# A fused two-stage window attention and long-convolution kernel: entry and stage ends reordered, fewer fillers, the first attention block in four groups of whole rows

## The chip, the cores and the metric

The kernel runs on one core of a Trainium2 chip. The metric is device time in microseconds (us) of one execution; 220.42 us is the median of three runs of the kernel before (219.79 to 220.80). The engines are TensorE (PE in the profile; PEld is its weight load), VectorE (DVE), ScalarE (ACT), GpSimd (POOL) and SyncE (SP), which here only issues DMAs. Each engine works through its own program in order, and the programs meet at semaphores.

## The reference

The input x has 32 channels and 56 x 56 pixels. Two residual steps follow one another:

```python
def _gn(v, G=32, eps=1e-05):      # norm of each channel over its image
...
x = x + _L0_conv_ref(_gn(x), ...)  # two attention blocks
x = x + _L1_conv_ref(_gn(x), ...)  # long convolution, GLU, layer norm, decoder
```

The first step is a window attention (block stage, "b": 8 x 8 windows of 7 x 7 neighbouring pixels), then a grid attention (stage "g": 7 x 7 windows of 8 x 8 pixels). Each has 4 heads of 8 channels, a bias table by relative position, a softmax, a projection with residual, a layer norm over the 32 channels and a feed-forward of 128 with the norm's output as its shortcut. The second step encodes 32 channels to 256, convolves each with 16 taps that come from a small state-space model, applies GELU, a gated linear unit, a residual, a layer norm over 256, and decodes to 32 channels.

## The kernel before

**Stages.** The whole image lies in SBUF. The kernel goes through: entry (loads, first group norm, first q/k), block stage (to about 71 us), grid stage (to about 130 us), second group norm and the start of the convolution (to 136), convolution with GELU (to 165), GLU with norm and decoder in seven chunks of 448 pixels (to the end). To keep precision at half-precision matmul speed, many operands are split in a half-precision part ("hi") and a half-precision remainder ("lo").

**Entry.** The group norm takes its sums from `xq`, four quarters of x_win side by side (loads L416 on SP, L801 on ACT). DVE forms the statistics (L1082 to L1088), after it made the key tables, with two copies into `ones` (L1192). The selection table `sel` (L418, third in SP's queue) gives `repeat32` (L1199), with which PE sums the quarters (L1796). ACT turns the result into scale and offset `gr` (L824 to L829). Then `x1`, which comes in three pieces (PIECES, L40; loads L425 on SP for rows 0 to 63 and L808 on ACT for rows 64 to 95), is normed in four window pieces of 784 columns: ACT writes the hi copy (`window_hi`, L841), someone writes the full copy into `u32` (`window_f32`: DVE for piece 0, L1313, ACT for pieces 1 to 3, L847), and the lo part is their difference (`window_lo`: DVE for piece 0, POOL for pieces 1 to 3, L678). The q/k matmul of window row r (L1593) needs the lo part. POOL also makes the bias halves (`split_bias`, L542), which the scores need, and issues the loads of p1, par_g and w_glu.

**Attention in groups.** `strips` (L315) lists the groups: two strips of windows are worked on at once in the two halves of the partitions. In the block stage groups 0 to 2 hold two whole window rows (8 windows wide), groups 3 and 4 one window row each, cut in two halves of 4 windows. `groups`, `rows_of`, `halves_of` and the use of the PSUM banks (`ring_uses`, L354) follow from the list. For each group g PE's loop (L1822 to L1861) runs the second orientation of the scores of two heads (`turned_scores`, L1648), values, the projection of the group before, the scores of the next group, the other two heads, the variance of the group before, then the attention sums in one or two halves (`attend`, L1688), the q/k of later rows and the feed-forward of the group before. ACT's loop (L978 to L1009) runs exp (L885), the log and exp that invert the row sums (L898, L900), and the norm's square, log and exp (L913, L921, L928). DVE's loop (L1384 to L1427) takes the row maxima (L1225), the q/k splits (L1178), the outputs (L1255), the norm's output (L1266) and puts finished rows back in image order (L1285).

**Feed-forward.** `feed_forward` (L1742) uses two half-precision matmuls on the parts that POOL makes (`norm_halves`, L696) for all groups but the last, and one full-precision matmul for the last (L1762), so that no wait for POOL stands there.

**Fillers.** `keep_running(n)` (L1766) issues n matmuls of 512 columns on a zero tile, whose result is not used. They stand in places where PE would be idle.

**After the grid stage.** DVE's second group norm gives `gr`. The first chunk's shifted copies in `u4hi` are written by ACT (rows 0 to 63, L1022) and DVE (L1439), and the lo parts in `u4lo` by DVE (s = 0, 1, L1448) and POOL (s = 2, 3, L753). All later chunks are shifted by DMAs from `ust_s` (L449, L457, L760), in the segments of L39. At the end, for the last chunk, the order on PE is L2011 to L2018, with the sums of squares in `mean_square` (L1928) inside `decode(last)`, and DVE's is L1541 to L1546.

## Time and profile before

| | us |
|---|---|
| median of three runs | 220.42 |
| profiled execution, its own time | 220.49 |
| its span, first to last instruction | 218.7 |
| PE busy | 197.0 (90%) |
| DVE busy | 151.2 (69%) |
| ACT busy | 128.7 (59%) |
| POOL busy | 102.5 (47%) |
| all fillers on PE (114) | 34.8 |
| mean granted TensorE clock | 0.966 |

The profile comes from one execution; its time lies within the three runs. Busy shares are over the whole span. A wait is named after the instruction whose semaphore came last. In timeline rows the first two numbers are the start and the length of a merged run of instructions, the brackets hold the idle time before it and who ended it.

### The profile page before, as it was taken

To read this page: it belongs to the slowest core of one execution; us is meant where nothing else is said; L and a number is where in the kernel's file an instruction comes from. 1 tells how busy PE (TensorE), PEld (TensorE's weight loads), DVE (VectorE), ACT (ScalarE), POOL (GpSimd) and SP (SyncE) were. 2 spreads that over 40 slices of the span, in tenths; PEclk is the share of its full clock that TensorE was granted. 3 is DMA by queue.
4 is the path that set the end of the run, shared out by engine and by line. 5 is a ranking of instruction groups with operands and counts; after the bars stand their busy time and mean duration, and the time that the engine had idled before them with its cause. 6 is when DMAs were issued, how large, how long until landed. Compare 5 with 4: busy or idle time off the path is not lost.

```text
span 218.7 us, 6364 instructions
## 1 busy us (share of the span) xinstructions
PE 197.0 (90%) x2563; PEld 102.9 (47%) x2563; DVE 151.2 (69%) x300; ACT 128.7 (59%) x248; POOL 102.5 (47%) x221
## 2 busy tenths in 40 slices
PE   7698789989898799898989796999999999999995
PEld 2254334435553244344344343445555556666582
DVE  8777486947664676739878789963323768898873
ACT  2373986775574737765636619755448665656650
POOL 7258562737860313767895504410000466577540
PEclk9889999999999799999999999999999999999975
DMA  6765500000000000020000000460000000000000
GB/s 181 168 155 121 113 4 4 4 3 3 3 3 0 0 3 3 17 86 1 3 4 0 3 0 12 95 146 2 0 0 0 3 0 3 13 11 13 11 11 21
DMA packets 3841, 6.70 MB, mean 31 GB/s; under 512 B 1605, under 2 KB 2773, under 8 KB 3717
## 3 DMA queue, kind: packets, MB, share of 16 engines
q1 hardware_dynamic: 2581, 3.91, 7.8%
q0 software_dynamic: 560, 1.48, 2.7%
q10 hardware_dynamic: 672, 0.92, 1.7%
q8 instruction: 20, 0.33, 0.7%
q14 instruction: 8, 0.07, 0.1%
HBM read 4.53 MB, written 0.40 MB: 23 GB/s over the span
## 4 chain that ended last, share of the span: by engine, by line
PE 65%; DVE 13%; ACT 11%; issue 4%; POOL 3%; DMA 2%; SPq 0%; DVEq 0%; ACTq 0%; POOLq 0%
PE ps L1923 15%; PE ps L1888 13%; PE ps L1769 5%; PE ps L1683 3%; DVE x L1285 3%; PE ps L1727 3%; PE ps L1739 2%; DMA sel<-pick 2%; PE ps L1704 2%; PE ps L1661 2%; PE ps L1673 2%; PE ps L1629 2%; PE ps L1709 2%; PE ps L1974 2%; PE ps L1593 2%
## 5 line engine op out<-in xcount | busy, mean ns | idle before, releaser
L1769 PE MATMUL ps<-fill 128*128 128x512 f16 x114 | 34.8, 429 | 1.8 <-DVE fill L1355 1.2
L1225 DVE TENSOR_REDUCE mx<-ps 128x16 f32<-128x784 f32 (+3 forms) x18 | 15.8, 888 | 15.2 <-PE ps L1643 15.2
L885 ACT ACTIVATE pr<-ps 128x784 f32<-128x784 f32 (+3 forms) x18 | 13.7, 761 | 12.0 <-PE ps L1683 11.9
L858 ACT CAST q_hi<-ps 128x392 f16<-128x392 f32 (+1 forms) x30 | 13.8, 512 | 11.3 <-PE ps L1593 10.9
L768 POOL TENSOR_TENSOR pr<-pr 128x448 f16<-128x448 f32 x7 | 7.4, 1063 | 27.0 <-ACT pr L1064 27.0
L1769 PEld LDWEIGHTS ps<-fill 128*128 128x128 f16 x114 | 10.8, 107 | 14.7 <-issue 4.9
L1040 ACT ACTIVATE pt<-ps,ybias 128x448 f32<-128x448 f32 x14 | 8.9, 637 | 12.9 <-PE ps L1888 12.0
L1285 DVE STREAM_TRANSPOSE x<-u 96x448 f32<-96x448 f32 (+4 forms) x12 | 13.9, 1154 | 2.0 <-ACT u L938 1.7
L1923 PE MATMUL ps<-vm_buf,wglu_hi 128*128 128x448 f16 x56 | 15.1, 352 | 0.0
L1888 PE MATMUL ps<-u4hi,gw_hi 128*128 128x448 f16 x56 | 12.9, 353 | 1.5 <-ACT u4hi L1022 1.5
L1064 ACT CAST pr<-pr 128x448 f16<-128x448 f32 x14 | 7.9, 566 | 10.0 <-DVE pr L1519 10.0
L1467 DVE TENSOR_TENSOR vm_buf<-pt,qs 128x448 f16<-128x448 f32 x7 | 4.4, 624 | 13.3 <-ACT qs L1042 13.3
L692 POOL TENSOR_TENSOR ust_g<-x,ust_g 32x448 f16<-32x448 f32 x5 | 5.1, 1026 | 17.1 <-ACT ust_g L947 17.0
L1704 PE MATMUL ps<-pr,ones 128*32 128x196 f32 (+2 forms) x120 | 8.5, 354 | 5.1 <-DVE on L1255 3.8
L1888 PE MATMUL ps<-u4hi,gw_lo 128*128 128x448 f16 x56 | 12.9, 352 | 0.0
L1178 DVE SCALAR_TENSOR_TENSOR qs<-q_hi,cst,ps 128x392 f16<-128x392 f16 (+1 forms) x15 | 9.7, 646 | 4.4 <-ACT q_hi L858 4.1
L1888 PE MATMUL ps<-u4lo,gw_hi 128*128 128x448 f16 x56 | 11.7, 352 | 0.5 <-POOL u4lo L753 0.5
L1512 DVE SCALAR_TENSOR_TENSOR pt<-ps,p,pt 128x448 f32<-128x448 f32 x14 | 9.6, 683 | 3.4 <-ACT pt L1056 1.8
L773 POOL TENSOR_TENSOR pr<-pr 128x448 f32<-128x448 f32 x6 | 6.8, 1134 | 9.4 <-ACT pr L1065 9.4
L1255 DVE TENSOR_TENSOR on<-ps,rec 128x196 f32<-128x196 f32 (+2 forms) x15 | 5.6, 375 | 7.1 <-ACT rec L900 7.1
L898 ACT ACTIVATE den<-ps 128x196 f32<-128x196 f32 (+2 forms) x15 | 5.2, 349 | 8.9 <-PE ps L1709 8.7
L1519 DVE SCALAR_TENSOR_TENSOR pr<-ps,p,pt 128x448 f32<-128x448 f32 x14 | 9.6, 683 | 0.5
(275 smaller groups left out, 531.9 us busy)
## 6 DMA issues: line engine op xcount, KB each, us to landing
xr<-x SPq DMA_DIRECT2D x3, 392.0 KB, 5.5
wglu<-w_glu POOLq DMA_DIRECT2D x1, 512.0 KB, 4.4
x<-x_win SPq DMA_DIRECT2D x4, 112.0 KB, 3.9
out<-u SPq DMA_DIRECT2D x7, 56.0 KB, 1.6
x<-x_win SPq DMA_DIRECT2D x2, 168.0 KB, 5.2
u4hi<-ust_s SPq DMA_DIRECT2D x4, 84.0 KB, 2.6
par_g<-stage_g POOLq DMA_DIRECT2D x1, 274.5 KB, 3.1
x<-x_win ACTq DMA_DIRECT2D x2, 112.0 KB, 6.1
```

The costliest lines, as they stand in the source:

```text
L858: nc.scalar.copy(q_hi[:, i % 4, 0:cw], qk_bank(k, i)[:, 0:cw]).then_inc(s_qkhi[k], 1)
L885: nc.scalar.activation(dst[:, :, 0:cw], ps[:, 2:4, 0:cw], ACT.Exp).then_inc(s_exp[k], 1)
L1040: nc.scalar.activation(gy[n % 2][a], ps[:, i % 4, 0:CW], ACT.Gelu_apprx_tanh, bias=ybias[:, a:a + 1])
L1178: nc.vector.scalar_tensor_tensor(out=dst[:, r * cw:(r + 1) * cw], in0=q_hi[:, i % 4, 0:cw], scalar=const(low), in1=qk_bank(k, i)[:, 0:cw], ...
L1225: nc.vector.tensor_reduce(m[:, :, 0:n], ps[:, bank:bank + 2, 0:n * T].rearrange("p h (j m) -> p h j m", m=T), AX.X, ALU.max).then_inc(s_mx ...
L1285: nc.vector.transpose(x1[:, :].rearrange("p (c k) -> p k c", c=C)[:, first:last, :], u32[:, first * C:last * C].rearrange("p (k c) -> p k ...
L1512: nc.vector.scalar_tensor_tensor(out=ag[a], in0=ps[:, VALUE[a], 0:CW], scalar=s4("bglu")[:, a:a + 1], in1=sg[a], op0=ALU.add, op1=ALU.mult ...
L1519: nc.vector.scalar_tensor_tensor(out=rr[n % 2][a], in0=ps[:, ENC[a], 0:CW], scalar=s4("benc")[:, a:a + 1], in1=ag[a], op0=ALU.add, op1=ALU ...
L1704: nc.tensor.matmul(ps[32 * h:32 * h + 32, 6, 256:256 + w], weights, p[:, h, first * T:last * T], start=True, stop=True)
L1769: nc.tensor.matmul(ps[:, bank, :], fill[:, 0:128], fill[:, :], start=True, stop=True)
L1888: ins = nc.tensor.matmul(ps[:, i % 4, 0:CW], wt[:, j, a * 128:(a + 1) * 128], ut[:, at:at + CW], start=(first and j == 0), stop=(last and ...
L1923: ins = nc.tensor.matmul(ps[:, bank, 0:CW], wt[:, b, o:o + 128], yt[b][:, c], start=(m == 0), stop=(m == 5))
```

## The change

It touches ten places.

1. SP issues the load of `sel` before its two quarters, and no longer loads rows 0 to 63 of piece 1; POOL does, behind its memsets and ahead of its wait for piece 0, on a semaphore of its own.
2. The window pieces: piece 0's hi copy is made in two halves on ACT, and its lo part in two halves on DVE; the full copy of piece 1 is made on POOL, in front of `split_bias("b")`; ACT makes hi copy 2 and full copy 2 ahead of the group loop, and hi copy 3 ahead of the first group's second exp.
3. The two copies into `ones` go from DVE's first work to `pick_tables`, behind the lo parts.
4. Fillers: 11 and 6 instead of 9 and 4 around the group norm, none of the three that stood behind the first hi copy; 8 instead of 5 before the grid q/k; none inside block groups 1 and 2; none before the grid's last projection.
5. `strips["b"]`: four groups of two whole window rows.
6. `halved_norm`: in the grid stage groups 0 and 1 use the half-precision feed-forward, group 2 the full-precision one; POOL's `norm_halves("g", 2)` goes.
7. In the grid stage's end PE runs the first feed-forward before the last projection.
8. The lo part of s = 2 goes from POOL to DVE.
9. In the tail PE computes the first sum of squares of the last chunk before a `decoded_back`, and two fillers go from behind the last `decode` to in front of it.
10. In the tail DVE scales chunk 5 before it waits for the last sums of squares.

```diff
@@ strips
-                        [(6, 0, 4), (6, 4, 4)], [(7, 0, 4), (7, 4, 4)]],
+                        [(6, 0, 8), (7, 0, 8)]],
...
+        def halved_norm(k, g):
+            return g < groups[k] - (1 if k == "b" else 2)
@@ block.sync
+            sp.dma_start(sel[:, :], pick).then_inc(s_sel, 16)
             for q in range(2):
                 sp.dma_start(xq[32 * q:32 * q + 32, :],
                              x_win[:, q * (PX // 4):(q + 1) * (PX // 4)]).then_inc(s_xq, 16)
-            sp.dma_start(sel[:, :], pick).then_inc(s_sel, 16)
...
-                    image_piece(1)
                     image_piece(2)
@@ block.gpsimd
+            def window_f32(n):
+                c = slice(n * 784, (n + 1) * 784)
+                pool.wait_ge(s_gnr, 3)
+                pool.wait_ge(s_x[n], 16)
+                pool.wait_ge(s_xp, 32)
+                step(nc.gpsimd.tensor_scalar(u32[32:64, c], x1[32:64, c], gr[32:64, 0, 0:1], gr[32:64, 0, 1:2],
+                                             ALU.mult, ALU.add))
...
+            pool.wait_ge(s_padz, 1)
+            first, last = PIECES[1]
+            for i in range(2):
+                pool.dma_start(x1[32 * i:32 * i + 32, first * CW:last * CW],
+                               x_win[:, first * CW:last * CW]).then_inc(s_xp, 16)
             pool.wait_ge(s_x[0], 48)
             pool.dma_start(p1[:, 0:256], s4d[:, 0:256]).then_inc(s_par, 16)
             pool.dma_start(p1[:, 256:S4D_W], s4d[:, 256:S4D_W]).then_inc(s_par, 16)
+            window_f32(1)
             split_bias("b")
...
-            norm_halves("g", 2)
...
-            for s in range(2, 4):
-                nc.gpsimd.tensor_tensor(u4lo[32 * s:32 * s + 32, PAD + s:PAD + s + CW], u32[64:96, 0:CW],
+            nc.gpsimd.tensor_tensor(u4lo[96:128, PAD + 3:PAD + 3 + CW], u32[64:96, 0:CW],
@@ block.scalar, window_hi
+                for c in ((slice(0, 392), slice(392, 784)) if n == 0 else (c,)):
+                    nc.scalar.activation(ust["b"][:, c], x1[:, c], ACT.Identity, bias=gr[:, 0, 1:2],
+                                         scale=gr[:, 0, 0:1]).then_inc(s_uhi["b"], 1)
@@ block.scalar, program
                     window_hi(1)
-                    window_f32(1)
                     decay_exponents()
-                    for i in range(4, 8):
+                    window_hi(2)
+                    for i in range(4, 6):
+                        qk_hi("b", i)
+                    window_f32(2)
+                    for i in range(6, 8):
                         qk_hi("b", i)
...
                     if k == "b" and g == 0:
-                        window_hi(2)
-                        window_f32(2)
+                        window_hi(3)
...
-                    if k == "b" and g == 0:
-                        window_hi(3)
@@ block.vector
+            def window_lo():
+                dve.wait_ge(s_u32, 1)
+                for r in range(2):
+                    c = slice(r * 392, (r + 1) * 392)
+                    dve.wait_ge(s_uhi["b"], r + 1)
+                    nc.vector.tensor_tensor(ust["b"][32:64, c], u32[32:64, c], ust["b"][32:64, c],
+                                            ALU.subtract).then_inc(s_ulo["b"], 1)
...
-            for s in range(2):
+            dve.wait_ge(s_firstd, 1)
+            for s in range(3):
...
                 if n == NCH - 1:
+                    token_scale(n - 1)
                     dve.wait_ge(s_z, n + 1)
...
-            token_scale(last - 1)
             token_scale(last)
@@ block.tensor, entry
-            keep_running(9)
-            pe.wait_ge(s_const, 2)
+            keep_running(11)
+            pe.wait_ge(s_const, 1)
...
-            keep_running(4)
+            keep_running(6)
             pe.wait_ge(s_gnr, 3)
             keep_running(5)
-            pe.wait_ge(s_uhi["b"], 1)
-            keep_running(3)
...
-                    keep_running(5)
+                    keep_running(8)
@@ block.tensor, groups
-                    keep_running(1)
+                    dense = k == "b" and g in (1, 2)
+                    if not dense:
+                        keep_running(1)
                     if len(halves_of(k, g)) > 1:
                         attend(k, g, 1)
-                    keep_running(2)
+                    if not dense:
+                        keep_running(2)
...
-                keep_running(2)
-                project(k, last)
                 if k == "b":
+                    keep_running(2)
+                    project(k, last)
                     keep_running(1)
                     variance(k, last)
-                for r in rows_of(k, last - 1):
-                    feed_forward(k, r)
-                if k == "g":
+                    for r in rows_of(k, last - 1):
+                        feed_forward(k, r)
+                else:
+                    first, second = rows_of(k, last - 1)
+                    feed_forward(k, first)
+                    project(k, last)
+                    feed_forward(k, second)
                     variance(k, last)
@@ block.tensor, tail
             decode(last - 1)
             mean_square_of_sum(last - 1)
+            pe.wait_ge(s_sg, 2 * last + 1)
+            pe.wait_ge(s_ag, 2 * last + 1)
+            pe.wait_ge(s_rq, 2 * last + 1)
+            mean_square(last, 0)
             decoded_back(last - 2)
+            keep_running(2)
             decode(last)
-            keep_running(2)
             decoded_back(last - 1)
```

## Rows read from the trace of the kernel before

**Rows 1.** Chain of waits, entry: start, length, what (merged).

```profile
8.73 3.16 PE ps L1769 x8
...
14.85 1.05 ACT u L849
15.98 1.67 POOL ust_b L683
```

**Rows 2.** Timeline, ACT, 16 to 21 us: start, length, operation [idle before, releaser].

```profile
18.14 0.88 ACT L858 CAST q_hi<-ps 128x392 f16<-128x392 f32 x2 [1.92 <-PE ps L1593]
20.57 0.88 ACT L858 CAST q_hi<-ps 128x392 f16<-128x392 f32 x2 [1.54 <-PE ps L1593]
```

**Rows 3.** Timeline, DVE and POOL, entry.

```profile
1.59 3.92 DVE L1192 COPY ones<-key_of 128x32 f32<-128x32 f32 x2
...
8.55 0.58 POOL L711 DMA_DIRECT2D p<-s4d  x1 [3.11 <-DMA x<-x_win]
...
10.85 0.21 DVE L1124 COPY wpr_b<-par_b 32x128 f32<-32x128 f32 x1
...
11.87 1.07 POOL L552 TENSOR_TENSOR bt_b<-bias,bt_b 49x196 f16<-49x196 f32 x2
```

**Rows 4.** Busy time by stretch, block stage: stretch, length, engines, clock, DMA share, GB/s.

```profile
30.70:41.60 10.90, 10.18 (x257) 4.87 (x256) 8.68 (x20) 7.56 (x17) 5.32 (x18) 1.00 0.02 5
41.60:51.30 9.70, 8.77 (x223) 4.57 (x221) 6.00 (x11) 6.45 (x15) 5.04 (x18) 1.00 0.01 2
51.30:59.80 8.50, 7.78 (x149) 4.29 (x147) 5.68 (x12) 4.84 (x12) 6.63 (x21) 1.00 0.02 4
59.80:71.10 11.30, 10.25 (x132) 5.18 (x129) 6.02 (x13) 6.48 (x16) 4.02 (x17) 1.00 0.01 1
```

**Rows 5.** Groups by form, 28 to 72 us: busy us, mean ns, idle before.

```profile
L900 ACT ACTIVATE rec<-den 128x196 f32<-128x196 f32 x7 | 2.6, 368 | 0.2
...
L1225 DVE TENSOR_REDUCE mx<-ps 128x8 f32<-128x392 f32 x4 | 2.3, 567 | 4.2 <-PE ps L1643 4.1
...
L1225 DVE TENSOR_REDUCE mx<-ps 128x16 f32<-128x784 f32 x2 | 1.9, 970 | 1.8 <-PE ps L1643 1.8
```

**Rows 6.** Timeline, PE, last feed-forward of the block stage.

```profile
68.60 0.90 PE L1762 MATMUL ps<-yn,affz_b 64*96 64x196 f32 x4 [0.25 <-DVE yn L1266]
```

**Rows 7.** Busy time by second: PE, PEld, DVE, ACT, POOL, clock, DMA share, GB/s.

```profile
9.00:10.00 1.00, 1.00 (x5) 0.33 (x4) 0.64 (x2) 0.75 (x1) 0.67 (x2) 0.61 0.41 58
...
71.00:72.00 1.00, 0.00 (x0) 0.00 (x0) 0.37 (x2) 0.86 (x2) 0.00 (x0) 1.00 0.00 0
...
74.00:75.00 1.00, 1.00 (x5) 0.43 (x3) 1.00 (x3) 1.00 (x3) 0.00 (x0) 0.53 0.00 0
...
131.00:132.00 1.00, 0.08 (x1) 0.00 (x0) 0.97 (x2) 0.97 (x2) 0.00 (x0) 1.00 0.00 0
...
210.00:211.00 1.00, 1.00 (x16) 1.00 (x15) 0.97 (x4) 1.00 (x1) 0.00 (x0) 0.80 0.00 0
```

**Rows 8.** Timeline, DVE and ACT, end of the grid stage.

```profile
122.12 0.68 DVE L1277 SCALAR_TENSOR_TENSOR u<-ps,cvec_g,xr 96x448 f32<-96x448 f32 x1 [1.25 <-PE ps L1759]
...
124.04 0.41 ACT L928 ACTIVATE rstd<-lnv 64x256 f32<-64x256 f32 x1
```

**Rows 9.** Timeline, POOL, PE and PE's weight load, start of the convolution.

```profile
133.51 2.65 POOL L753 TENSOR_TENSOR u4lo<-u,ust_s 32x448 f16<-32x448 f32 x2 [7.92 <-ACT ust_s L1027]
...
136.31 1.67 PE L1888 MATMUL ps<-u4lo,gw_hi 128*128 128x448 f16 x8 [0.50 <-POOL u4lo L753]
...
137.92 0.49 PEld L1888 LDWEIGHTS ps<-u4hi,gw_hi 128*128 128x128 f16 x4 [0.38 <-DMA u4hi<-ust_s]
```

**Rows 10.** Timeline, POOL and PE, tail.

```profile
211.66 1.01 POOL L779 TENSOR_TENSOR rs<-veps,neghalf 112x4 f32<-112x4 f32 x1 [2.68 <-DVE veps L1487]
...
213.04 1.01 PE L1769 MATMUL ps<-fill 128*128 128x512 f16 x2
```

**Rows 11.** DMA issues, page: queue, count, KB each, median us to landing.

```profile
x<-x_win ACTq DMA_DIRECT2D x2, 112.0 KB, 6.1
```

More of the change, by code:

```diff
@@ L1189, in key_rows @@
                 ins.then_inc(s_key, 1)
-                dve.wait_ge(s_key, 1)
-                for i in range(2):
-                    ins = nc.vector.tensor_copy(ones[:, i, :].rearrange("p (r w d) -> p r w d", r=2, w=2),
-                                                key_of[:, i, :].unsqueeze(1).unsqueeze(3).broadcast_to([128, 2, 2, 8]))
-                ins.then_inc(s_const, 1)
             def pick_sums():
@@ L1207, in pick_tables @@
             def pick_tables():
+                dve.wait_ge(s_key, 1)
+                for i in range(2):
+                    ins = nc.vector.tensor_copy(ones[:, i, :].rearrange("p (r w d) -> p r w d", r=2, w=2),
+                                                key_of[:, i, :].unsqueeze(1).unsqueeze(3).broadcast_to([128, 2, 2, 8]))
+                ins.then_inc(s_const, 1)
                 dve.wait_ge(s_const, 3)
@@ L1361, in _ @@
                     window_f32(0)
-                    window_lo(0)
+                    window_lo()
                     spread_projection("b")
@@ L1748, in feed_forward @@
                 pe.wait_ge(s_affz[k], 3)
-                if g < groups[k] - 1:
+                if halved_norm(k, g):
                     pe.wait_ge(s_ynl[k], g + 1)
@@ L1754, in feed_forward @@
                     out_at = ring_bank(k, ("f", r))[0:96, j0 * T:(j0 + nj) * T]
-                    if g < groups[k] - 1:
+                    if halved_norm(k, g):
                         cols = yn2[:, g % 2, 0:nj * T]
```

72 lines of the change are left out of this document (32 added, 40 removed).

## The prediction

> **What bounds the kernel now.** I read the chain of waits first, stage by stage, since shares over the whole span mix stages with different limits. At the entry the chain hops from engine to engine [rows 1]: eight fillers on TensorE (PE), then the q/k casts, then one window piece in three steps (ACT makes the half-precision copy, ACT the full one, POOL the low part). Between 20.6 and 30 us ACT works without a gap and is the limit, after it had stood idle twice shortly before [rows 2]. What DVE and POOL do at the entry is in [rows 3]. In the block attention each group is a round trip PE, ACT, DVE, PE; its stretches are in [rows 4], pieces of the round trip in [rows 5], the last feed-forward in [rows 6]. The granted clock is in [rows 7]: it fell at 9, at 74 and at 210 us. The end of the grid stage hangs on DVE, once PE has given the first feed-forward [rows 8]. The convolution starts behind POOL's low part, and its second chunk behind a transfer [rows 9]. From there to the decoder's last chunk PE runs on its own, and the change leaves that alone. The end is a ping-pong of small operations at the low clock [rows 10]. How long an image piece takes to land is in [rows 11].
>
> **Base.** The sum is made against the profiled execution: span 218.7, 220.49 with what lies around it (1.8). The median of the three runs, 220.42, is the same within a measurement.
>
> **Entry.** (1) The selection table goes first in SP's queue, the two quarters behind it are issued 0.4 later, and the copies of `ones` that lay before the statistics go away. The scale of the first norm comes perhaps 0.5 earlier. But POOL saw the first image piece only at 8.55 [rows 3], 0.1 before that scale was there, and nothing moves the piece forward. Worth 0.1; ends 0 and 0.6. (2) PE issues five fillers there instead of eight. At 395 ns each (3.16 for eight [rows 1]) that is 1.2 less. The first q/k then waits for the fillers (8.6+2.0=10.6) and no longer for a low half of 784 columns, since the first piece is now cut in two on ACT and DVE. It stood at 11.7, so 1.0 with (1). (3) Piece 1: ACT's full copy (1.05 [rows 1]) leaves the chain; POOL does it earlier, beside the fillers. The trace has no such operation on POOL. Its nearest rows are POOL's 784-column subtraction, 1.66 [rows 1], as the upper bound, and ACT's copy of the same columns, 1.05, as the value, since it too reads one input; the lower bound is half the subtraction, 0.8. It ends near 11, before the two low halves of the bias start at 11.87 [rows 3], so the bias keeps its time, 12.9. POOL's low part then starts behind ACT's half copy, at 13.9 instead of 15.98: 2.05 earlier. (4) Two more ACT operations (piece 2, 2.1) move out of the gapless run into ACT's two waits of 1.92 and 1.54 [rows 2]. What is late next is the bias: 12.9, its matmul 0.45, four fillers 0.9, so the first scores come at 14.4 instead of 15.1. The first exp comes about 1.5 earlier, the second, with one operation less in front, 2.5. Taken for the entry as a whole: **2.4**. Ends: 0.9 (only step 2) and 3.9 (steps 2 to 4 in full). Queued behind POOL's new waits are the bias halves, for which PE waits. Two DMA issues (0.6 each, as [rows 3]) go in front of POOL's wait for the image piece, a stretch of 3.1 us in which it did nothing.
>
> The copies of `ones` come back on DVE behind the low halves, at about 10.5. A copy alone took 0.21; the pair took 3.92 while POOL had memsets [rows 3]. Now they meet POOL's window piece and bias casts, and the first q/k split would be held by what is left of one such operation: 0 to 1.7, typically half. The bias gate of (4) leaves 0.6 of slack, so I book nothing, and 1.0 as the far end. The Trainium skill, SBUF — State Buffer, section Who interferes with whom, states that such a copy on VectorE and a GpSimd instruction exclude each other for a whole instruction. By that rule the new place is a bad one, and the sum would be up to 1.0 higher; by the row of the lone copy it stays. The trace agrees with the rule in the 3.92 us.
>
> **Block attention.** Before: stretches of 10.9, 9.7, 8.5 and 11.3 from the second group on [rows 4], the last two with a half-wide group each, the last with the drain. After: the 10.9 stays; the fillers taken out of groups 1 and 2 lie in waits for DVE, so they give nothing. The 9.7 becomes 10.1: the next group's scores are full width (0.2 per pair of heads) and its maxima 0.97 instead of 0.57 [rows 5]. The last group starts as the half-wide one did at 59.8 and is longer by: wider bias, scores and projection on PE 1.5; the norm of the group before, now full width on ACT, 0.25; a whole second half of attention, 0.9 on PE, then three steps of 0.37 (one of them in [rows 5]), 2.05 with latencies; a norm chain over 392 instead of 196 columns, five steps of 0.2, 1.05; two full-precision feed-forwards of 392 columns instead of one (0.90 [rows 6]), 0.8; the second row's drain 0.15. That is 5.8 on 11.3, 17.1. Sum 10.9+10.1+17.1=38.1 against 40.4: **2.3** gained. Ends 1.2 (DVE's fold of the grid weights now stands in a full-width group) and 3.5.
>
> **Grid entry.** Eight fillers for five leave PE idle for 1.5 instead of 1.8 us before the first q/k. Before, the clock fell to 1.2 GHz at 74 us [rows 7], and four fillers and the first scores took about 1.0 longer. PE was as idle at 131 us without a fall [rows 7]. Between 0 and 1.0, taken **0.5**.
>
> **Grid end.** Two fillers and the projection (0.65) leave the way of the first feed-forward, which is now full precision (0.9) instead of two halves (0.55). It starts at 120.1 and ends at 121.0, so DVE's residual, which stood at 122.12 behind a wait of 1.25 [rows 8], starts 1.1 earlier. But the last norm's scale comes where it did, at 124.45 [rows 8], so DVE then waits 0.4 for it: **0.6** is left; ends 0 and 1.1.
>
> **Convolution start.** One of two POOL operations (2.65 both [rows 9]) goes to DVE. PE's wait of 0.5 goes, but the second chunk waits for the shifted transfer already [rows 9], and that comes no sooner. **0.1**; ends 0 and 0.6.
>
> **Tail.** Two fillers (1.01 [rows 10]) no longer stand before the last-but-one transposes. POOL's scale of chunk 5 is ready at 212.67 [rows 10] and now stands before the last variance on DVE; that waits for PE's sums, which end at 213.0, anyway. The last transposes still wait for the last scale, so half is left: **0.5**; ends 0 and 1.6, the latter if the clock stays up at 210 and only POOL's 212.67 bounds.
>
> **Sum.** 2.4+2.3+0.5+0.6+0.1+0.5=6.4, span 212.3, time 214.1. All lower ends give 2.1, time 218.4.
>
> **Rivals.** (A) *The clock stays up* at the grid entry and at the end: 0.5 and 1.1 more, 212.5. For it: more fillers at both places. Against it: the fall at 210 came while PE was busy all the second [rows 7]. (B) *The entry is held by its transfers*: POOL's rows of piece 1 land late, and the bias halves queue behind them. The slow image pieces took 6.1 us from issue [rows 11]; issued at 6, POOL's would land past 12, and the bias halves end at 15 to 16 instead of 12.9. The entry then gives between 0.5 and minus 1.5: 216 to 218. Against it: the DMA share is down to 0.41 after 9 us [rows 7]. (C) *The merged group does not pay*: its last round trip grows by all that the fifth group saves: 216.4. (D) *Slower*: the groups without fillers lose the clock. Place: the stretches from 30.7 to 51.3, where PE is busy for 10.18 and 8.77 us [rows 4]. At 1.2 GHz these grow by up to 19, more likely half: 224. It decides against the change once over 6.4 us are added, a third of them. Against it: without the three fillers (0.65) PE is still busy for 87% of the first stretch, while the fall at 74 came after a second with 0.00 [rows 7].
>
> **Chances.** The forecast 0.58, A 0.12, B 0.20, C 0.06, D 0.04. The range goes from A with a little of the upper ends, 211.0, to most of B, 217.6. A change under 0.5% (1.1 us) can't be told from none. Faster by more: forecast, A, C and all of B but its far end, 0.94; within: 0.02; slower: 0.04.
>
> **What would show it.** Right: a lead of some 2.4 us by the second block group; 16 row maxima on DVE instead of 18; PE's gap before the grid q/k near 1.5; DVE's residual of row 4 released by a full-precision feed-forward; PE waiting for the transfer, not for POOL, in the convolution's first chunks. Wrong: POOL waiting for image rows before its window piece; copies of over 1 us on DVE at 10 us; a low clock between 30 and 50 us; a last block group of over 18 us with its drain.

## The result: 0.7% faster, a quarter of the forecast

The changed kernel took 220.11 us in the median of 20 runs (216.99 to 223.78), the kernel before 220.69 in 20 runs (219.14 to 221.72). The ratio is 0.993, with an interval of 0.990 to 0.995: 1.6 us faster, where 6.3 were forecast. The ratios, here and below, leave out slow executions (most of them over 1.5% above the fastest of their kernel: nine of the changed kernel's twenty, none of the other's), while medians and ranges count all, and by the medians the gain is 0.6 us. The changed kernel scatters over 6.8 us where the one before scatters over 2.6, and that scatter turns out to be part of the story. Below, a ratio is always to the kernel before; as 0.01 is 2.2 us and an interval reaches 0.003 to 0.006 to each side, kernels less than 1 us apart can't be told from one another.

The profiled execution of the changed kernel took 221.40, its span is 219.6: a bad one for it, 1.3 above its median. It lies 0.9 above the 218.7 of before, and it shows where the gain went; what it alone shows need not hold for the kernel's better executions.

### The profile page after: what moved, and what is told of

Same layout as the page of the kernel before. It is cut to its first block, busy times and chain, and to the rows that moved or that the text cites. A ratio compares the mean times of both kernels' runs of the same rounds, so it can differ in the third digit from the quotient of the medians.

```text
span 219.6 us, 6264 instructions
## 1 busy us (share of the span) xinstructions
PE 196.8 (90%) x2530; PEld 100.5 (46%) x2530; DVE 146.4 (67%) x297; ACT 126.3 (58%) x241; POOL 101.0 (46%) x219
## 4 chain that ended last, share of the span: by engine, by line
PE 60%; DVE 14%; ACT 8%; issue 6%; SPq 4%; DMA 3%; POOL 3%; POOLq 1%; DVEq 0%
PE ps L1917 13%; PE ps L1952 12%; DVE x L1303 3%; PE ps L1707 3%; PE ps L1751 3%; PE ps L1793 3%; PE ps L1685 3%; PE ps L1728 2%; PE ps L1763 2%; SPq L441 2%; DMA bias<-tab_b 2%; PE ps L1697 2%; PE ps L1653 2%; PE ps L1733 2%; PE ps L1667 2%
## 5 line engine op out<-in xcount | busy, mean ns | idle before, releaser
L1793 PE MATMUL ps<-fill 128*128 128x512 f16 x107 | 32.1, 427 | 1.2 <-DVE fill L1378 1.2
L1243 DVE TENSOR_REDUCE mx<-ps 128x16 f32<-128x784 f32 (+2 forms) x16 | 15.5, 980 | 14.4 <-PE ps L1667 14.4
L906 ACT ACTIVATE pr<-ps 128x784 f32<-128x784 f32 (+2 forms) x16 | 13.3, 833 | 14.8 <-PE ps L1707 14.7
L879 ACT CAST q_hi<-ps 128x392 f16<-128x392 f32 (+1 forms) x30 | 13.7, 511 | 9.1 <-PE ps L1617 8.8
L1793 PEld LDWEIGHTS ps<-fill 128*128 128x128 f16 x107 | 10.1, 105 | 14.4 <-issue 4.9
L1061 ACT ACTIVATE pt<-ps,ybias 128x448 f32<-128x448 f32 x14 | 8.9, 633 | 12.9 <-PE ps L1917 12.0
L1917 PE MATMUL ps<-u4hi,gw_hi 128*128 128x448 f16 x56 | 12.9, 353 | 2.1 <-ACT u4hi L1043 1.5
L1303 DVE STREAM_TRANSPOSE x<-u 96x448 f32<-96x448 f32 (+4 forms) x12 | 13.5, 1155 | 0.9 <-ACT u L959 0.7
L1085 ACT CAST pr<-pr 128x448 f16<-128x448 f32 x14 | 7.9, 564 | 10.1 <-DVE pr L1544 10.1
L1491 DVE TENSOR_TENSOR vm_buf<-pt,qs 128x448 f16<-128x448 f32 x7 | 4.4, 624 | 13.3 <-ACT qs L1063 13.3
L1917 PE MATMUL ps<-u4hi,gw_lo 128*128 128x448 f16 x56 | 12.9, 353 | 0.0
L718 POOL CAST yn<-yn 64x392 f16<-64x392 f32 (+1 forms) x5 | 2.6, 521 | 15.9 <-DVE yn L1284 11.0
```

Source lines behind the costliest of these rows:

```text
L879: nc.scalar.copy(q_hi[:, i % 4, 0:cw], qk_bank(k, i)[:, 0:cw]).then_inc(s_qkhi[k], 1)
L906: nc.scalar.activation(dst[:, :, 0:cw], ps[:, 2:4, 0:cw], ACT.Exp).then_inc(s_exp[k], 1)
L1061: nc.scalar.activation(gy[n % 2][a], ps[:, i % 4, 0:CW], ACT.Gelu_apprx_tanh, bias=ybias[:, a:a + 1])
L1085: nc.scalar.copy(rr_hi[n % 2][a], rr[n % 2][a]).then_inc(s_rhi, 1)
L1243: nc.vector.tensor_reduce(m[:, :, 0:n], ps[:, bank:bank + 2, 0:n * T].rearrange("p h (j m) -> p h j m", m=T), AX.X, ALU.max).then_inc(s_mx ...
L1303: nc.vector.transpose(x1[:, :].rearrange("p (c k) -> p k c", c=C)[:, first:last, :], u32[:, first * C:last * C].rearrange("p (k c) -> p k ...
```

## The profile after, beside that of before

**The entry.** First DVE, POOL and PE in the timelines of the changed kernel.

```profile
6.24 1.03 DVE L1103 BATCH_NORM_STATS2 stats_q<-xq 128x6 f32<-128x392 f32 x2 [4.68 <-DMA xq<-x_win]
...
11.90 0.24 DVE L1224 COPY ones<-key_of 128x32 f32<-128x32 f32 x2
...
12.42 0.80 DVE L1230 SCALAR_TENSOR_TENSOR mask<-col_of,half_of 128x16 f32<-128x16 f32 x1
```

```profile
12.11 1.09 POOL L688 TENSOR_SCALAR u<-x,gr 32x784 f32<-32x784 f32 x1 [2.56 <-DMA bias<-tab_b]
13.26 0.64 POOL L552 CAST bt_b<-bias 49x196 f16<-49x196 f32 x2
13.98 1.08 POOL L556 TENSOR_TENSOR bt_b<-bias,bt_b 49x196 f16<-49x196 f32 x2
...
16.04 1.69 POOL L697 TENSOR_TENSOR ust_b<-u,ust_b 32x784 f16<-32x784 f32 x1
```

```profile
15.21 0.50 PE L1653 MATMUL ps<-bt_b,sel 128*128 128x392 f16 x2 [1.10 <-POOL bt_b L556]
```

The statistics start at 6.24, 2.1 later than before (4.09): the two quarters now stand behind the selection table in SP's queue. POOL waits for transfers until 12.11, where the forecast had it start its copy near 10. Its bias halves, which began at 11.07 and 11.87 [rows 3], begin at 13.26 and 13.98, and PE has the bias at 15.21. POOL's low part of piece 1 starts at 16.04, where it stood at 15.98 [rows 1]. So the entry gives nothing. POOL's copy needs the image rows, not the table; the bias table's last packet reports at 12.69 in the trace, while POOL is at that copy.

The same second, 8 to 9 us, in the queues of the two kernels: packets, MB, and the share of the 16 DMA engines. SP's queue is q1, POOL's is q0. Before:

```profile
q10 hardware_dynamic: 107, 0.08, 39.8%
q1 hardware_dynamic: 134, 0.02, 17.4%
```

After:

```profile
q0 software_dynamic: 26, 0.14, 60.6%
q10 hardware_dynamic: 144, 0.07, 43.5%
q1 hardware_dynamic: 71, 0.01, 9.9%
```

At that time SP's queue carries the bias table, in small packets. Beside 26 large packets of POOL's image rows it gets 71 through instead of 134. Run 12 repeats this with that one edit.

**The block stage.** PE's timeline at the end of the first group, then busy time by stretch of the last three groups, each from its second orientation of the scores to the next (the last one to the grid stage's first hi copy; columns as in [rows 4]).

```profile
27.67 0.34 PE L1733 MATMUL ps<-pr,vm_buf 128*32 128x49 f32 x13
29.45 0.46 PE L1733 MATMUL ps<-pr,vm_buf 128*32 128x49 f32 x19 [1.44 <-issue]
```

```profile
31.32:43.22 11.90, 10.47 (x256) 5.02 (x254) 8.74 (x20) 7.88 (x18) 4.30 (x13) 0.92 0.01 3
43.22:54.34 11.12, 9.92 (x258) 5.42 (x257) 7.07 (x16) 6.70 (x14) 5.49 (x19) 0.97 0.01 3
54.34:74.34 20.00, 18.07 (x214) 7.19 (x212) 8.13 (x14) 10.00 (x21) 9.73 (x34) 0.84 0.00 1
```

PE stops for 1.44 us in the middle of the attention sums, after 13 of 32 equal matmuls whose inputs are all there. Nothing released it; "issue" is all that the profile says. Then the stretches: 11.9, 11.1 and 20.0, together 43.0, against 40.6 before between the same events (40.4 in [rows 4], which start 0.2 later) and 38.1 in the forecast. The clock column says why it is not 38: 0.92 and 0.84, where all four of before had 1.00. By the second:

```profile
29.00:30.00 1.00, 0.55 (x20) 0.45 (x21) 0.63 (x2) 0.06 (x1) 0.91 (x2) 0.91 0.02 8
30.00:31.00 1.00, 1.00 (x4) 0.31 (x3) 0.29 (x1) 0.64 (x2) 0.70 (x4) 0.50 0.06 16
...
53.00:54.00 1.00, 0.64 (x3) 0.47 (x4) 0.63 (x4) 0.41 (x2) 0.76 (x4) 0.86 0.00 0
54.00:55.00 1.00, 1.00 (x4) 0.30 (x2) 0.93 (x6) 0.93 (x2) 0.75 (x4) 0.50 0.00 0
```

From 29.8 to 33.2 and from 53.7 to 60.5 the granted clock is at 0.50, which is 1.2 GHz. The same four matmuls, in group 2 at the full clock and in group 3 at half:

```profile
43.98 0.52 PE L1707 MATMUL ps<-mxe,negsel 64*49 64x392 f16 x4
...
55.61 0.85 PE L1707 MATMUL ps<-mxe,negsel 64*49 64x392 f16 x4
```

**The rest.** Grid entry, grid end, the first chunk's low part, and the tail:

```profile
75.69 1.07 PE L1617 MATMUL ps<-ust_g,wst_g 96*128 96x448 f16 x4 [1.52 <-DVE ust_g L1329]
...
122.46 0.99 PE L1786 MATMUL ps<-yn,affz_g 64*96 64x448 f32 x2
...
214.75 0.93 PE L1998 MATMUL ps<-cst,zt 112*32 112x112 f32 x4 [1.15 <-DVE zt L1501]
```

```profile
123.49 0.68 DVE L1295 SCALAR_TENSOR_TENSOR u<-ps,cvec_g,xr 96x448 f32<-96x448 f32 x1 [0.36 <-PE ps L1786]
...
126.82 0.49 DVE L1284 SCALAR_TENSOR_TENSOR yn<-ps,pbc_g,rstd 64x256 f32<-64x256 f32 x1 [0.35 <-ACT rstd L949]
```

```profile
134.29 0.49 PEld L1917 LDWEIGHTS ps<-u4hi,gw_hi 128*128 128x128 f16 x4 [1.98 <-ACT u4hi L1043]
...
139.60 0.49 PEld L1917 LDWEIGHTS ps<-u4hi,gw_hi 128*128 128x128 f16 x4 [1.03 <-DMA u4hi<-ust_s]
```

PE's gap before the grid q/k is 1.52, and no fall follows; before, the clock fell there [rows 7]. DVE's residual waits 0.36 instead of 1.25 [rows 8], and then DVE waits 0.35 for the last norm's scale, as worked out. In the convolution the wait for POOL's low part is gone and the one for the transfer is there. In the tail the last transposes but one wait for DVE behind POOL's scale.

The whole difference, as distances between the same events in both profiles (us; the events are the second orientation of the scores of a group, the grid's first hi copy, the first convolution and the first GLU matmul):

| stretch | before | after | difference | forecast |
|---|---|---|---|---|
| start to block group 0 | 18.98 | 19.32 | +0.34 | |
| group 0 to group 1 | 11.54 | 12.00 | +0.46 | both: -2.4 |
| group 1 to grid's first hi copy | 40.62 | 43.02 | +2.40 | -2.3 |
| to grid group 0 | 8.23 | 7.24 | -0.99 | -0.5 |
| grid group 0 to group 3 | 33.78 | 33.93 | +0.15 | 0 |
| to the first convolution | 19.46 | 18.79 | -0.67 | -0.6 |
| to the first GLU matmul | 32.73 | 32.67 | -0.06 | -0.1 |
| to the end of the span | 53.36 | 52.63 | -0.73 | -0.5 |

Everything behind the block stage came out as forecast or better (2.3 for 1.7). Everything up to its end came out 7.9 us worse than forecast in this execution. The experiments are about that part.

## The experiments

Eighteen kernels ran, each of them six or twelve times, as edits of the changed kernel unless another is named. Each has one profile, of one execution. Beside the ratio I give the total time that the profiled execution spent at the lower clock before 200 us ("low"). It is 6.8 us for the kernel before (the falls at 9 and at 74 us in [rows 7]) and 13.7 for the changed one. It leaves out the start: until the clock's first recorded rise, at 4.0 to 6.4 us in most profiles, the views say 1.00, but the eleven fillers from 1.18 us take 444 ns each in run 5, and six at 7.72 take 243. In run 13 the first rise comes at 10.5 and in run 18 at 13.5, so that their entries ran at the lower clock for longer than "low" says.

**1. The selection table behind the quarters again.**

```diff
-            sp.dma_start(sel[:, :], pick).then_inc(s_sel, 16)
             for q in range(2):
                 sp.dma_start(xq[32 * q:32 * q + 32, :], ...).then_inc(s_xq, 16)
+            sp.dma_start(sel[:, :], pick).then_inc(s_sel, 16)
```

> The changed kernel with SP's loads in the order of before (two quarters, then the selection table). Queue theory (the quarters waited behind the table in SP's queue): the first statistics move from 6.24 back to about 4.1-4.7 us, the group-norm scale from 9.78 to about 8.7, and the first q/k from 11.95 to about 11.0; the lead of 0.9 stays only if the bias follows. Rival (the bias is bound by the image rows on POOL's queue, not by the scale): scale at 8.7, but bias halves still end at 14.5 to 15.1, first scores still after 16.2, time unchanged within 0.5 us of the changed kernel (fast runs about 218.5-219).

Measured 220.67 us, ratio 0.999 (0.996 to 1.003), low 10.2: if anything slower than the changed kernel, though the statistics start at 4.21 and the first q/k at 10.69, 1.3 us earlier. PE then waits:

```profile
15.19 0.50 PE L1653 MATMUL ps<-bt_b,sel 128*128 128x392 f16 x2 [2.63 <-POOL bt_b L556]
```

The rival holds: the table costs 2 us at the statistics, but the bias comes at 15.19, where the changed kernel has it at 15.21. By the ratios the run is 1.4 us slower than the changed kernel, more than the rival's 0.5. What was gained in front became a gap of 2.63 us, and the clock was at half from 16 to 22.8.

**2. POOL's full copy of piece 1 behind the bias halves.**

```diff
-            window_f32(1)
             split_bias("b")
+            window_f32(1)
```

> The changed kernel with POOL's full copy of piece 1 behind the bias halves instead of in front of them. If the window piece and its late rows hold the bias (rival B): bias halves end near 12.9-13.9 instead of 15.06, first scores at 14.4-15.2 instead of 16.50, POOL's low part of piece 1 about where it was (16.0), and 0.5 to 1.3 us gained. If the bias table's own landing (12.1) holds it: bias halves end at 14, first scores at 15.4. If the clock theory alone explains the shortfall, nothing beyond 0.3 us is gained at the end.

Measured 219.28, ratio 0.993 (0.989 to 0.996), low 10.2. POOL's first bias cast now waits for its own data, and only for that:

```profile
13.33 0.64 POOL L552 CAST bt_b<-bias 49x196 f16<-49x196 f32 x2 [3.75 <-DMA bias<-tab_b]
```

So most of the 1.09 us of POOL's copy hid behind the table's landing. What holds the bias is the table, which lands at 13.3 here instead of at 11.07 [rows 3]; none of my cases had it that late. The landing varies: in the trace of the changed kernel it is 12.69, and there the copy, which could not start before 12.11, held the bias for another half microsecond. In all eight profiles in which POOL issues the rows the last landing is between 12.6 and 13.3; in the twelve in which SP does, the kernel before among them, it is between 10.8 and 12.0.

**3. The fillers back in block groups 1 and 2** (`dense = False`).

> The changed kernel with the three fillers back inside block groups 1 and 2. Clock theory (rival D in part): the granted clock no longer falls at 53.7 us (it was at half until 60.5), the last block group with its drain takes about 17.4 instead of 20.0 us, and the times scatter less, median 218 or below. Rival (the clock falls for another reason, for instance the wait for POOL's norm halves): the fall at 50 to 60 us is still there in the profile, the time the same within 0.5 us, or 0.3 us longer by the fillers themselves.

Measured 219.02, ratio 0.993 (0.989 to 0.996), low 13.7: no difference to the changed kernel. There was no fall at 53.7, but one from 31.8 to 42.0, behind a stall of 1.95 us at the same attention sums; group 1 took 15.3 us. So the missing fillers are not what loses the clock, as far as one profile and equal ratios can say, and that takes the mechanism from rival D. With the clock up the last group took 17.4.

**4. The kernel before with the merge alone** (the four groups in `strips`).

> The kernel before with the first block in four groups and nothing else changed. By the prediction's sum: stretches of 10.9, 10.1 and 17.1 us instead of 10.9, 9.7, 8.5 and 11.3, 2.3 us faster, 218.4 against 220.7. If the merged group does not pay (rival C): 220.2 to 221. If the clock falls here too, between 53 and 61 us, though the fillers are in: 220 to 222, and the clock loss belongs to the merge and not to the fillers.

Measured 220.05, ratio 0.996 (0.992 to 0.999), low 10.2, with falls at 8.9, 19.2 and 73.8. Two groups of the new form stand in it at the full clock: 10.8 and 17.4 us, against 9.7 and 19.8 of before from group 2 to the grid stage. So the merge is worth 1.3 us by the profile and 0.9 by the ratio, not 2.3.

**5. As 2, and the image rows of piece 1 back in SP's queue behind the bias table.**

```diff
@@ block.sync
                 if k == "g":
+                    image_piece(1)
                     image_piece(2)
@@ block.gpsimd
...
-            pool.wait_ge(s_padz, 1)
-            first, last = PIECES[1]
-            for i in range(2):
-                pool.dma_start(x1[32 * i:32 * i + 32, first * CW:last * CW], ...).then_inc(s_xp, 16)
```

> The kernel of the run before it (full copy of piece 1 behind the bias halves) with the rows of piece 1 back in SP's queue, behind the bias table. Transfer theory: POOL's image rows run beside the bias table's small packets and hold its landing at 13.3 us; with them gone the table lands near 11, POOL's halves start at 11 to 11.3 and end at 12.6 to 13.2, the first scores come near 14.9 instead of 17.2, PE's gap before the bias matmul is under 0.3, and the first exp comes 1.0 to 2.0 us earlier. Rival (the table is late because the selection table stands ahead of everything in SP's queue): it lands at 13 still. Whether the clock falls near 16 us tells whether the fall belongs to PE's gap.

Measured 216.35, ratio 0.982 (0.979 to 0.985), low 0.0. This one edit gives 2.4 us on top of run 2, more than the whole change had given, and five of its six times lie within 0.8 us (the sixth is 219.75). POOL, PE, and the queues from 8 to 9 us:

```profile
10.88 0.97 POOL L552 CAST bt_b<-bias 49x196 f16<-49x196 f32 x2 [1.72 <-DMA bias<-tab_b]
```

```profile
13.29 0.50 PE L1645 MATMUL ps<-bt_b,sel 128*128 128x392 f16 x2 [0.55 <-POOL bt_b L556]
```

```profile
q10 hardware_dynamic: 142, 0.07, 40.8%
q1 hardware_dynamic: 165, 0.03, 20.0%
```

SP's queue gets 165 packets through, the table lands at 10.88. The stretches of the block stage, all at the full clock:

```profile
18.80:29.59 10.79, 9.49 (x254) 4.72 (x254) 7.82 (x16) 8.16 (x16) 6.20 (x15) 1.00 0.52 117
29.59:40.97 11.38, 9.68 (x256) 4.75 (x254) 9.04 (x21) 7.72 (x18) 5.47 (x18) 1.00 0.02 4
40.97:51.78 10.81, 9.61 (x257) 5.30 (x256) 6.78 (x15) 6.41 (x14) 5.26 (x18) 1.00 0.01 3
51.78:69.22 17.44, 15.53 (x215) 6.52 (x212) 8.39 (x17) 10.18 (x20) 9.96 (x35) 1.00 0.00 1
```

From group 1 on they take 39.6 together, 1.0 under before. Against my expectation the first exp did not come earlier (21.39 for 21.32), but the second block group did, by 0.9.

**6. The residual loads late.** SP loads the residual image three times, right behind the grid's bias table, and that waits for POOL's bias halves.

```diff
+            sp.wait_ge(s_on["b"], 1)
             for i in range(3):
                 sp.dma_start(xr[32 * i:32 * i + 32, :], x).then_inc(s_xr, 16)
```

> The changed kernel with SP's three loads of the residual image held until the first attention output (about 30 us). Fetch theory: PE's stall of 1.44 us at 28.0 (in the middle of the attention sums, released by nothing) is its instruction fetch behind these loads, which ran until 27 us there and until 25 before. Then the stall is gone or under 0.5, the first stretch of the block stage takes 11.0 instead of 12.0, and there is no fall of the clock at 30: 1.0 to 2.0 us gained where the fall went with it. Rival (a fetch that is late by the program's own length): the stall stays at 28.

Measured 219.47, ratio 0.987 (0.983 to 0.990), low 13.7. By the ratio it is 1.4 us faster than the changed kernel, with intervals that just meet. It has no stall, but the profile can't decide: the clock fell at 16.3 in this execution, and PE came to the place 3 us later, when the loads of the changed kernel would have been over too. The question went to runs 13 and 14.

**7. Both cures, the table behind the quarters, and rows 4 and 5 finished early** (their feed-forwards in front of the last projection, `block_out` in front of the last square, their transposes in front of the last norm).

> The changed kernel with the full copy of piece 1 behind the bias halves, its rows on SP, the selection table behind the quarters, the residual loads late, and rows 4 and 5 of the block finished ahead of the last norm (their feed-forwards before the last projection, their transposes before the last norm on DVE). If the causes add: scale at 8.6, first scores at 14.5, no stall at 28, last block group with drain 17.0 instead of 17.4; time 216 to 217 in fast runs, 3.5 to 4.5 below before. If the clock decides alone: 218 to 219 with the same scatter.

Measured 216.46, ratio 0.982 (0.979 to 0.985), low 3.4: no better than run 5. The last group with its drain took 17.3 for 17.4. The transposes of rows 4 and 5 looked serial in the drain of the changed kernel, but the full-precision feed-forward of the last rows, 1.55 us, ends at the same time. The lowest time of all runs is here, 215.48.

**8. The kernel before with the later parts alone** (grid entry, grid end, low part, tail).

> The kernel before with only the later parts of the change: eight fillers before the grid q/k, the grid stage's new end, the low part on DVE, the tail's new order. By the profile of the changed kernel these stretches gave 1.0 (grid entry), 0.7 (grid end), 0.1 and 0.7 (tail): 2.0 to 2.5 below before, 218.2 to 218.7, with before's small scatter. If the clock's falls there were chance and not the fillers: 1.0 to 1.3 below, 219.2 or more.

Measured 219.36, ratio 0.995 (0.992 to 0.998), low 3.4. Its profile has the gains of the table (grid entry 7.24 for 8.23, grid end 18.88 for 19.46, tail 52.56 for 53.36), 2.1 us by its span, and the runs show half of it. It may be that some of these gains come only in executions in which the clock stays up; no run tests that.

**9. Run 5 with the selection table behind the quarters.**

> The kernel with piece 1's rows back on SP, with the selection table again behind the two quarters. If the table's place costs on top of the rows (queue theory): statistics at 4.1 to 4.7 us instead of 5.8, scale 0.7 to 1.3 earlier, and the first scores at 14.4 or sooner if the scale holds them: 0.2 to 0.6 us faster, 215.8 to 216.2. If the bias table's landing is the only gate: first scores at 14.8 as they are, no difference over 0.3.

Measured 217.86, ratio 0.988 (0.983 to 0.993), low 10.2: not faster. As in run 1 the q/k came earlier (10.18), the bias did not (13.22), the gap between them grew to 1.17, and the clock fell at 14.2.

**10. Run 5 with five groups in the block stage.**

> The kernel with piece 1's rows back on SP, with the first block in five groups as before (groups 1 and 2 without fillers). By the stretches with the clock up (9.7 and 19.8 against 10.8 and 17.4) the merge is worth 1.3 us: 217.6 to 217.8. By the prediction's sum 2.3: 218.7. If the merge gives nothing (rival C): 216.1 to 216.7.

Measured 217.44, ratio 0.986 (0.982 to 0.990), low 3.4. From group 2 to the grid stage it takes 9.6 and 19.8, 29.4 against 28.3 in run 5: the merge gives 1.1 by the profile, 0.9 by the ratios, whose intervals overlap. Neither 2.3 nor nothing.

**11. Run 5 with five fillers before the grid q/k.**

> The kernel with piece 1's rows back on SP, with five fillers instead of eight before the grid stage's first q/k. If the three fillers keep the clock up there: PE's gap is 1.8 to 2.2 instead of 1.5, the clock falls at 72 to 74 us, and the stretch from the first grid q/k to the second orientation of the scores takes 6.9 instead of 5.9: 1.0 us slower, 217.3. If they don't matter: the clock stays up in this run too, no difference over 0.3.

Measured 217.99, ratio 0.987 (0.982 to 0.992), low 3.4. PE's gap was 2.15 us, but in this profile the clock stayed up behind it and the stretch took 7.24, as with eight. The fall was elsewhere, at 40.5. In run 4 the same gap of 2.15 was followed by a fall. The fillers' worth stays open.

**12. The kernel before, with the rows of piece 1 issued by POOL and nothing else.**

> The kernel before with one thing of the change: the rows of piece 1 are issued by POOL behind its memsets instead of by SP behind the bias table. Transfer theory: the bias table lands at 12.5 to 13.3 instead of 11.0, the halves end at 14.5 to 15, the first scores come at 16.3 to 17, and the kernel is slower than before by 1 to 3 us (the fall of the clock behind PE's gap included), 221.5 to 223.5, with a wider scatter. Rival (the rows alone do nothing; the later landing came from the rest of the new entry): bias at 11, time 220.2 to 220.9.

Measured 222.23 in the median (218.98 to 225.37), 1.8 above the kernel before; the ratio is 1.001 (0.997 to 1.006), so the loss sits in the scatter, which went from 2.9 to 6.4 us. Low 10.2, with a new fall at 26. POOL's first bias cast and, from 8 to 9 us, SP's queue, with this edit alone:

```profile
12.91 0.64 POOL L548 CAST bt_b<-bias 49x196 f16<-49x196 f32 x2 [2.78 <-DMA bias<-tab_b]
...
q1 hardware_dynamic: 62, 0.01, 10.1%
```

The table lands 1.8 us later than in [rows 3], and SP's queue gets 62 packets through instead of 134.

**13 and 14. A bridged gap, with and without early residual loads.** Both have five fillers in PE's gap before the first bias matmul; 14 has the late loads of run 6 as well.

```diff
                 if k == "b":
                     fold("b")
+                    keep_running(5)
```

> The changed kernel with five fillers (1.1 us at the full clock) in PE's gap before the first bias matmul, where PE waits 1.10 us for POOL; bias and scores come no earlier. Clock theory (the gap makes the clock fall in part of the executions, right behind it or some us later): median 217.5 to 218.5 instead of 220.1, fewer times above 220. Rival (the late bias costs by itself, the clock falls whatever stands there): 219.5 to 220.5, the same scatter from 217 to 224. The stall of 1.44 us at 28 should be there in both.

> The same five fillers, and SP's three residual loads held until the first attention output. Fetch theory: where PE is at the attention sums at 28 us, as in the changed kernel, the stall of 1.44 us is gone (or under 0.4) and the first stretch of the block stage takes 10.9 to 11.0; 0.5 to 1.5 us faster than the bridged kernel. Rival: the stall is there, no difference.

Run 13 took 219.60, ratio 0.988 (0.982 to 0.994), low 10.2; run 14 took 217.18, ratio 0.983 (0.978 to 0.988), low 3.4. In both profiles PE is at the same matmuls at the same time. First 13, then 14:

```profile
27.56 0.27 PE L1733 MATMUL ps<-pr,vm_buf 128*32 128x49 f32 x8
29.86 0.47 PE L1733 MATMUL ps<-pr,vm_buf 128*32 128x49 f32 x24 [2.03 <-issue]
```

```profile
27.31 0.54 PE L1734 MATMUL ps<-pr,vm_buf 128*32 128x49 f32 x32
```

With the loads early PE stops for 2.03 us, with the loads late it does not stop at all; groups 0 to 3 begin at 19.2, 31.1, 44.9 and 56.4 in the one, and at 19.0, 29.5, 40.6 and 51.4 in the other. In run 13 the clock is at half from 31.0 to 37.8, right behind the stall. PE's instructions are what it probably waited for. In the changed kernel the queues show, from 26.5 to 28.5 us:

```profile
q1 hardware_dynamic: 42, 0.29, 67.8%
q8 instruction: 1, 0.02, 4.1%
q14 instruction: 1, 0.01, 2.2%
```

Instruction packets go through there, beside 0.29 MB of residual rows. In runs 13 and 14 the packet of q8 moves with the loads. Run 13 from 23 to 25, from 25 to 27 and from 27 to 29 us, then run 14 from 23 to 25:

```profile
q1 hardware_dynamic: 50, 0.41, 102.5%
...
q1 hardware_dynamic: 47, 0.39, 89.1%
...
q8 instruction: 1, 0.02, 4.1%
q14 instruction: 1, 0.01, 1.4%
q1 hardware_dynamic: 15, 0.00, 0.8%
```

```profile
q8 instruction: 1, 0.02, 3.0%
```

With the loads early no instruction packet passes between 23 and 27; it comes from 27.3 to 28.6, once the loads are over. With the loads late it comes at 23.6. In the traces of the changed kernel and of runs 3, 5, 13 and 15 PE goes on 1.2 to 1.6 us after the end of this packet. That it is PE's the profile doesn't say. Each side of the comparison is one profile, and those with a stall of over 1 us (221.40, 221.83, 221.47 and 219.59 us) are all of executions above their kernel's median. So what the stall costs in a median execution is not shown: the ratios of 13 and 14, as of 15 and 16 below, overlap. The bridge itself shows nothing certain: 0.988 against the changed kernel's 0.993, with intervals that overlap.

**15 and 16. The bridge in the mended kernels**: 15 is run 9 with the bridge, 16 is 15 with late residual loads.

> Rows of piece 1 on SP, selection table behind the quarters, and five fillers in PE's gap of 1.17 us before the bias matmul. If that gap brought the fall of the clock at 14.6 us, it is gone and the time is 215.5 to 216.5 instead of 217.9. If the fall is chance: 217 to 218.5.

> Rows on SP, selection table behind the quarters, residual loads late, gap bridged. The candidate for the best: 215.2 to 216.2 if the clock stays up in most executions, else 216.5 to 217.5.

Run 15 took 217.99, ratio 0.986 (0.982 to 0.991), low 6.8; run 16 took 216.85, ratio 0.983 (0.979 to 0.986), low 3.4. The fall that run 9 had at 14.2 is gone in 15. But PE, now 0.8 us ahead of run 5 (first group at 18.04 for 18.80), stalls for 2.44 us in its attention sums, the longest of all, and the clock falls behind it, at 29.4:

```profile
26.39 0.27 PE L1725 MATMUL ps<-pr,vm_buf 128*32 128x49 f32 x8
29.09 0.52 PE L1725 MATMUL ps<-pr,vm_buf 128*32 128x49 f32 x24 [2.44 <-issue]
```

In 16 the stall is gone, and its second block group starts at 28.49. That is 2.0 us before the 30.52 of the kernel before: nearly the 2.4 that I had forecast for the entry.

**17. Run 5 with late residual loads. 18. The kernel before with late residual loads.**

> Rows of piece 1 on SP behind the bias table, full copy behind the bias halves, selection table first as in the changed kernel, residual loads late. If the causes share one gain (with the rows on SP the loads end by 25 us, before PE needs its instructions): as with the rows alone, 216.0 to 216.6, first stretch 10.5 to 10.8. If they add: 215.0 to 215.8.

> The kernel before with the residual loads held until the first attention output. Its first stretch of the block stage is 11.5 us, with no stall put down to the fetch. If the stall came with the change: no difference over 0.3 us, 220.3 to 220.9. If the kernel before pays for it as well (hidden in its waits): first stretch 11.0 and 0.5 to 1.0 us faster.

Run 17 took 217.13, ratio 0.984 (0.979 to 0.990): the two cures share one gain, since with the rows on SP the residual loads are over by 25.8 us and only 0.27 us of stall were left. Run 18 took 220.96, ratio 1.002 (0.999 to 1.005). The kernel before does not measurably pay for those loads; the stall came with the change.

## Why the prediction was wrong, step by step

**Entry: 2.4 forecast, -0.8 in the profile.** This is the step that failed: the bias was to keep its time, and its halves ended at 15.06 instead of 12.9. (1) said that the table's new place in SP's queue brings the scale 0.5 earlier; it brought the scale later, as the quarters stood behind the table's packets (the statistics start at 6.24, and at 4.21 in run 1, where the quarters come first). (3) said that POOL's copy ends near 11 and that the bias "keeps its time, 12.9". I took the table's landing as fixed. The rows, issued beside the bias table instead of behind it, held the table until 12.7 to 13.3, and runs 2, 5 and 12 show it from both sides; the copy, late by its rows, added at most half a microsecond. Rival B named the place, the late bias and the end of its halves at 15 to 16 (15.06 here), and priced the entry at 0.5 to minus 1.5, which holds -0.8; its mechanism was half right, since it had the halves wait for the rows and not for the table. It deserved more than 0.20, but its 216 to 218 misses the 220.11 too. My argument against it, a DMA share of 0.41 after 9 us, was read in the kernel in which those rows were not yet there. (2) alone came true: q/k at 10.69 in run 1, for 10.6, where the quarters come first.

**What no step had: the stall.** SP's later loads wait for the bias halves, so late halves push the bulk of the residual loads, which ended at 25.5 us before, to about 28, where PE stalled. I had counted "who waits for that" on PE and not on SP.

**The clock.** The forecast left the block stage at full clock, and rival D, which did not, got 0.04, tied to the missing fillers. Run 3 says it is not the fillers. Of the 20 profiled kernels, with one execution each, only run 5 has no time at the lower clock between its first rise, at 6.4, and 200 us, and the one before has 6.8, the changed one 13.7. The falls of 16.0 in run 1, 15.9 in run 2, 29.8 in the changed kernel and 31.0 in run 13 stand within 2 us behind a gap of 1.3 to 2.6 us; others (43 in run 1, 40 in run 11) have no such gap, and gaps of 1.52 (changed kernel) and 2.15 (run 11) at the grid entry had no fall. So a gap often stands in front of a fall here and decides nothing; what does stays open, and with it how much of the changed kernel's scatter each cause explains.

**Block attention: 2.3 forecast for the merge, 1.1 to 1.3 measured** at the full clock (runs 4, 5 and 10), and 0.9 by the ratios: the lower end of my bounds, 1.2. Right in mechanism, wrong in size: the stretch that I took as 10.1 is 10.8 in runs 4 and 5. The fold of the grid weights and, in run 5, a wait of 0.83 for POOL's norm halves fall into it; how the 0.7 divides between them is not shown. The 17.1 was 17.4. Rival C is out.

**Grid entry** 0.5 forecast and 1.0 in the profile, **grid end** 0.6 and 0.7, **convolution** 0.1 and 0.06, **tail** 0.5 and 0.7: right by this profile; run 8's times show about half of it. The grid entry's 1.0 is that of a clock that stayed up, which run 11 does not put down to the three fillers; that part may be luck. The copies of `ones` cost nothing in the changed kernel: both took 0.24 in their new place, with POOL idle. That was luck, since POOL was idle because the table was late. In run 5 the table is early, and POOL's bias halves, with DVE's low half, the copies and the mask beside them, took 2.27 us from first cast to end, against 1.82 in run 7, where DVE was past most of these: 0.45 us on the way of the bias. The Trainium skill, SBUF — State Buffer, section Who interferes with whom, states that VectorE instructions of some forms and GpSimd exclude each other for a whole instruction. The trace agrees, on another row: the mask, 0.30 us before, took 0.80 at 12.42 and ended at 13.22, as POOL's window copy ended at 13.20.

**In sum**, the mended kernel of run 5 has a span of 214.4 against a forecast of 212.3: of the rest 1.5 is the entry and 1.3 the block stage, with 0.7 back behind the block stage. The change held 4 us of gain, and one of its edits, the rows on POOL's queue, gave 2.4 of it back.

## What to carry to other kernels

Before a load is moved to another queue, list what is in flight beside it at its new time, and ask of each what waits for it; here a table in small packets suffered beside large rows, though it has only 38 KB. Follow the lateness on to the queue that waits for its consumer, since a bulk load that slides by 2 us can land, as it seems to have done here, on an instruction fetch. And an operation made earlier in front of an unmoved gate is only a longer gap: in runs 1 and 9 it made the kernel no faster at all.

## What the runs showed of the hardware that I had not expected

- An engine can stop inside a run of equal matmuls for 1.4 to 2.4 us, with nothing in the profile but "issue", shortly behind bulk loads; with the loads late it did not (one profile each, runs 13 and 14, 15 and 16).
- 26 packets of 0.14 MB in POOL's queue within a microsecond went with half as many small packets in SP's queue, 71 for 134 (62 in run 12), though it had needed only 17.4% of the DMA engines.
- The same program can have the clock's falls at different places in different executions: the changed kernel and run 6 issue the same work until the residual loads at 22.8 us, and the clock fell at 16.3 in the one profile of run 6 and not in that of the changed kernel. The scatter of a kernel's times (0.8 us for most of run 5, 6.8 for the changed kernel) told more of it than the median.
